# Indirect transfers of a routed mixture-of-experts kernel sent back to back: no spacing, no tile gates, three gather buffers, a last unit combined block by block

## What is computed

```python
x = x + 0.5 * ffn(layernorm(x))      # mixture of experts
x = x + attention(layernorm(x))      # RWKV mixing: projections, a scan over the 512 positions, a projection
x = x + 0.5 * ffn(layernorm(x))      # the same experts again
# ffn: softmax(x @ gate_w), the best 2 of 8 experts per token, their weights normalised, then for expert i
h = silu(x @ w1[i]) * (x @ w3[i])    # 128 -> 512
out += (h @ w2[i]) * weight_i        # 512 -> 128
```

## Time and profile before

| | us |
|---|---|
| median of three runs | 676.24 |
| lowest, highest | 674.56, 677.45 |
| the profiled execution | 672.78 |
| its span in the trace | 671.0 |
| PE busy / DVE busy / ACT busy / POOL busy | 528.1 / 412.7 / 319.7 / 297.2 |
| POOL idle before scatters, until an `h` gate opened (26 times) | 136.4 |
| POOL idle before gathers, until an `h` gate opened (21 times) | 27.4 |
| PE idle until an `h` was made (13 times) | 26.0 |
| DVE idle before combines, until a gather landed (14 times) | 63.3 |

### The profile page before, as it was taken

One profiled execution on the slowest core, in us unless ns is written; L12 is line 12 of the kernel. 1 busy time (PEld: TensorE's weight loads), 2 busy tenths in 40 slices (PEclk: granted clock), 3 DMA queues, 4 the chain that ended last, 5 costly groups with the idle time before them and its releaser, 6 DMA issues. The chain is left out here.

```text
span 671.0 us, 18790 instructions
## 1 busy us (share of the span) xinstructions
PE 528.1 (79%) x5866; PEld 482.5 (72%) x5866; DVE 412.7 (62%) x1218; ACT 319.7 (48%) x703; POOL 297.2 (44%) x499
## 2 busy tenths in 40 slices
PE   2136899993899889898999859989789999989500
PEld 1125799893788878677888749878789899879500
DVE  4845975221678789588897848859786443333311
ACT  5433754441484566654656615854645344334100
POOL 1270356666540550565405655046005555525543
PEclk9999999998799999998999959999799999999955
DMA  8943234442221221222211133111112324322311
GB/s 287 325 143 99 84 112 147 136 134 67 76 77 41 64 72 49 73 64 63 78 49 45 53 99 83 44 60 49 57 34 77 100 81 127 85 64 72 86 52 43
DMA packets 89016, 59.57 MB, mean 89 GB/s; under 512 B 10208, under 2 KB 82656, under 8 KB 88928
## 3 DMA queue, kind: packets, MB, share of 16 engines
q1 hardware_dynamic: 55248, 29.97, 15.3%
q0 software_dynamic: 8192, 16.79, 8.9%
q10 hardware_dynamic: 25488, 11.61, 5.9%
HBM read 28.65 MB, written 29.69 MB: 87 GB/s over the span
## 5 line engine op out<-in xcount | busy, mean ns | idle before, releaser
L694 POOL DMA_INDIRECT rows_in<-parts,slot x128 | 132.5, 1035 | 232.9 <-DVE h L1084 136.4
L1084 DVE TENSOR_TENSOR h<-sil,pb 128x512 f32<-128x512 f32 x177 | 120.9, 686 | 145.8 <-PE pb L1201 59.3
L1215 PE MATMUL py<-ffn_w,h 128*128 x1416 | 199.0, 284 | 13.6 <-ACT yrow L753 12.4
L1215 PEld LDWEIGHTS py<-ffn_w,h 128*128 128x128 f32 x1416 | 175.3, 195 | 20.0 <-issue 13.9
L1201 PE MATMUL pa<-rT,ffn_w 128*128 128x128 f16 (+1 forms) x1752 | 152.7, 234 | 36.8 <-DVE h L1084 26.0
L708 POOL DMA_INDIRECT yg<-rows_out,slot x128 | 123.8, 968 | 130.3 <-issue 53.6
L1201 PEld LDWEIGHTS pa<-rT,ffn_w 128*128 x1752 | 124.9, 100 | 52.6 <-issue 41.1
L1201 PE MATMUL pb<-rT,ffn_w 128*128 128x128 f16 (+1 forms) x1752 | 157.1, 233 | 0.1
L1201 PEld LDWEIGHTS pb<-rT,ffn_w 128*128 x1752 | 124.4, 99 | 7.6 <-issue 0.3
L768 ACT ACTIVATE sil<-pa 128x512 f32<-128x512 f32 x177 | 105.4, 595 | 42.6 <-PE pa L1201 32.8
L748 ACT ACTIVATE rT<-pT 128x512 f16<-128x512 f16 (+1 forms) x112 | 56.8, 508 | 92.5 <-PE pT L1188 81.2
(11 more groups left out here) (155 smaller groups left out, 442.0 us busy)
## 6 DMA issues: line engine op xcount, KB each, us to landing
rows_out<-yrow ACTq DMA_DIRECT2D x177, 64.0 KB
rin<-rows_in SPq DMA_DIRECT2D x65, 128.0 KB
rows_in<-zrow SPq DMA_DIRECT2D x34, 128.0 KB
shared<-in_w SPq DMA_DIRECT2D x16, 256.0 KB, 7.0
rin<-rows_in SPq DMA_DIRECT2D x47, 64.0 KB
rows_in<-zrow SPq DMA_DIRECT2D x2, 1472.0 KB, 12.2
xres<-in_x SPq DMA_DIRECT2D x4, 512.0 KB, 5.7
ffn_w<-in_w SPq DMA_DIRECT2D x8, 256.0 KB
```

Source lines behind the costliest of these rows:

```text
L694: pool.indirect_dma_start(rows_in[g][:], bass.IndirectOffsetOnAxis(ap=slot[:, c, at:at + 1], axis=0), parts[:, at, :], None).then_inc(s_sc ...
L1084: dve.tensor_tensor(h[:, t % RING, :], sil[:, t % 2, :], pb[t % 2][:], ALU.mult).then_inc(s_h, 1)
L1215: mm = pe.matmul(py[:], h[:, step % RING, at:at + T], w, start=(c == 0), stop=(c == FC - 1))
```

## The change

- `pace` is gone, and so are the gates: POOL sends the transfers in the order of `TRANSFERS`, as fast as it can. A transfer still waits for what it reads (slots, data, zero fill, stored results).
- `yg` has three buffers (`GSLOTS`), given out in the order of the gathers. The n-th unit waits for the combine of the (n-3)-th.
- The unit that comes last (D) is combined block by block: two gathers of a block land on a semaphore of their own, DVE adds them with two instructions, SP writes the 64 KB of this block.
- The costs of the planner are altered and the plan is built anew. Of 449 entries 134 keep their tile, most of the rest move by one tile, the furthest by four. The order of units in the gathers stays.

```diff
-UP, TURN, DOWN, COPY_T, COPY_Y, SILU, H = 0.67, 0.055, 0.92, 0.3, 0.28, 0.6, 0.69
-HOP, LAND, SEND, LOAD = 0.1, 4.0, 1.1, 3.0
-SLIP = {"dve": 6.0, "act": 3.1, "pe": 2.0}
-SPACE = 1.6
+UP, UP_ALONE, TURN, DOWN, COPY_T, COPY_Y, SILU, H = 0.66, 0.73, 0.055, 0.9, 0.3, 0.28, 0.6, 0.69
+HOP, LAND, SEND, LOAD = 0.1, 4.5, 1.1, 3.0
+SLIP = {"dve": 6.5, "act": 3.1, "pe": 1.4}
+SPACE = 1.55
...
-        yg = sb("yg", [P, UG, TOPK, JU, D])
+        yg = sb("yg", [P, GSLOTS, TOPK, JU, D])
...
+                    if (run, b) == GATHERS[-1]:
+                        for j in range(JU):
+                            sp.wait_ge(s_lastc, j + 1)
+                            sp.dma_start(ov[:, js, :][:, j, :], xres[:, js, :][:, j, :]).then_inc(s_out, 16)
+                        return
...
-                if (j, c) == (0, 0):
-                    before = [p[1:] for p in PLAN if p[1] == "gather" and p[3] == b]
-                    at_b = before.index(("gather", run, b))
-                    if at_b:
-                        pool.wait_ge(s_comb, count(("combine",), ("combine", before[at_b - 1][1], b)))
+                n = GATHERS.index((run, b))
+                if (j, c) == (0, 0) and n >= GSLOTS:
+                    pool.wait_ge(s_comb, count(("combine",), ("combine", *GATHERS[n - GSLOTS])))
...
-            for sent, (gate, name, *one) in enumerate(TRANSFERS):
-                wait(pool, s_h, gate)
-                wait(pool, s_pace, sent)
+            for _, name, *one in TRANSFERS:
                 if name == "scatter":
                     scatter(*one)
                 else:
                     gather(*one)
-                pool.memset(pace[:], 0).then_inc(s_pace, 1)
...
+            def combine_last(run, b):
+
+                u, js = units(run, b)
+                slot_ = (len(GATHERS) - 1) % GSLOTS
+                for j in range(JU):
+                    xj = xres[:, js, :][:, j, :]
+                    dve.wait_ge(s_last[j], 16 * TOPK)
+                    for c in range(TOPK):
+                        ins = dve.scalar_tensor_tensor(xj, yg[:, slot_, c, j, :],
+                                                       wts[:, c, u * JU + j:u * JU + j + 1], xj, ALU.mult, ALU.add)
+                        if c == 0:
+                            link(ins)
+                    ins.then_inc(s_lastc, 1)
```

More of the change, by code:

```diff
@@ L77 @@
 YSLOTS = 10
+GSLOTS = 3
 RING = 6
@@ L187, in tile @@
         q, half, _ = TILE_OF[t]
-        up1 = max(self.free["pe"], self.rT[q] + HOP, self.h.get(t - 2, 0.0) + HOP) + UP
+        up = UP if paired(t) else UP_ALONE
+        up1 = max(self.free["pe"], self.rT[q] + HOP, self.h.get(t - 2, 0.0) + HOP) + up
         if t > SKEW:
@@ L311, in ask, with in_use @@
         waiting.append([due, at, name, run, [(b, j, c) for b in units for j in range(JU) for c in range(TOPK)]])
+    def in_use(run, unit):
+        order = [p[2:] for p in plan if p[1] == "gather"]
+        n = order.index((run, unit))
+        return n >= GSLOTS and "combine" not in gathered[order[n - GSLOTS]].ends
     def send(tile, until):
         while True:
-            now = [w for w in waiting if w[1] <= until and not (w[2] == "gather" and any(
-                c.next() == "combine" for c in chains if c.unit == w[4][0][0] and gathered.get((c.run, c.unit)) is c
-                and c.run < w[3]))]
+            now = [w for w in waiting if w[1] <= until and not (w[2] == "gather" and in_use(w[3], w[4][0][0]))]
             at = max([free["pool"]] + [min((w[1] for w in now), default=until)])
@@ L385, in count @@
     return order.index(upto) + 1
+GATHERS = [p[2:] for p in PLAN if p[1] == "gather"]
 def run_of(t):
@@ L445, in macaron_kernel @@
         zrow = sb("zrow", [P, 2 * D], F16)
-        pace = sb("pace", [P, PACE], U8)
         e_desc = sb("e_desc", [P, JG, E])
@@ L558, in macaron_kernel @@
         s_yst = [sem(f"y_stored{i}") for i in range(YSLOTS)]
-        s_gat = [sem(f"gathered{b}") for b in range(UG)]
+        s_gat = [sem(f"gathered{i}") for i in range(GSLOTS)]
+        s_last = [sem(f"last_gathered{j}") for j in range(JU)]
+        s_lastc = sem("last_combined")
         s_comb = sem("combined")
@@ L665, in _ @@
             last_steps(step)
-            sp.wait_ge(s_out, 16 * B)
+            sp.wait_ge(s_out, 16 * (B - 1 + JU))
         @block.gpsimd
@@ L702, in gather @@
                         pool.wait_ge(s_yst[k], 16 * len(range(k, PEND[run], YSLOTS)))
[L703 to L707 removed]
+                n = GATHERS.index((run, b))
+                if (j, c) == (0, 0) and n >= GSLOTS:
+                    pool.wait_ge(s_comb, count(("combine",), ("combine", *GATHERS[n - GSLOTS])))
                 pool.indirect_dma_start(
[L709 to L710 removed]
+                    yg[:, n % GSLOTS, c, j, :], None, rows_out[SET[run]][0:PASS_STEPS[PASS[run]] * T, :],
+                    bass.IndirectOffsetOnAxis(ap=slot[:, c, at:at + 1], axis=0)).then_inc(
+                        s_last[j] if n + 1 == len(GATHERS) else s_gat[n % GSLOTS], 16)
             def every(run, units):
@@ L1088, in combine @@
                 u, js = units(run, b)
-                runs = [p[2] for p in PLAN if p[1] == "gather" and p[3] == b]
-                dve.wait_ge(s_gat[b], 16 * TOPK * JU * (runs.index(run) + 1))
+                n = GATHERS.index((run, b))
+                dve.wait_ge(s_gat[n % GSLOTS], 16 * TOPK * JU * (n // GSLOTS + 1))
                 for c in range(TOPK):
@@ L1106, in step @@
                 if name == "combine":
-                    combine(run, b)
+                    (combine_last if (run, b) == GATHERS[-1] else combine)(run, b)
                 if name in ("stats", "mstats"):
```

8 lines of the change are left out of this document (3 added, 5 removed).

## The result

| | us |
|---|---|
| before, median of four runs | 676.85 (674.56 to 677.63) |
| after, median of four runs | 868.48 (867.05 to 869.97) |
| ratio | 1.284, 95% interval 1.280 to 1.288 |
| the profiled execution of after, its span | 867.47, 865.7 |

What follows compares the result with a forecast made beforehand. The prediction took POOL's gathers to bound the end and PE's idle time the part before. Gains of 17.2 + 0.8 + 17 + 11.3 + 7.3 + 0 = 53.6 gave 619.2 for a profiled-like execution, 623 as median; range 609 to 643.

Steps and rivals of the forecast that it cites:

- Step 6: All POOL transfers sent at once, in bursts beside loads and stores: cost taken as 0, bounds 0 and +6 us.
- slower: Rival: bursts of transfers slow the loads and stores of the tiles, about 689 us; chance 0.03.
- Step 1: The tail: D's gathers wait only for tile 176's store, 17.2 us less; last block's combine and write, 0.8 less.
- The 0.8 for the last block: Behind the last gather: fewer DVE instructions and a smaller last write gain 0.8 us, bounds 0 and 2.2.
- Step 2: The stall after tile 34, where DVE and PE wait for run 0's gathers: 17 us saved, bounds 13 and 18.
- Step 3: Run 5: PE's wait for the first load, slow register load and low clock behind them; 11.3 us saved, bounds 4 and 14.
- The 4.5 for the register load: Run 5: the 7.2 us register load, beside seven loads landing at once, was to lose 4.5 us of excess.
- Steps 2 to 4 together: Stall after tile 34 (17), run 5 (11.3) and DVE's smaller waits for gathers (7.3): 35.6 us saved.
- Step 5: The new plan moves work by a tile or so: taken as 0, bounds -4 (gain) and +8 us.
- new stalls of PE with a fall of the clock: Sign that the forecast is wrong: such stalls standing between 175 and 475 us.
- Its sign for step 1: In the tail: D's gathers start 1.25 us apart, with 10 to 12 us between last store and last gather.
- its being locked out: Rival: POOL can't write descriptors where DVE is busy, 2.2 us per transfer, only the tail gained, 655 us; chance 0.05.

Runs made afterwards that it cites:

- e3: After, with a small memset behind each transfer that waits only for the memset before the last one (1.29 us between transfers); 876.77 us.
- e8: After, with a memset of 600 bytes behind each transfer, its wait long fulfilled (1.73 us between transfers); 642.26 us, ratio 0.953.
- e5: After, with the small memset, the wait for it and a second, long fulfilled wait before each transfer, no gates (1.87 us apart); 663.96 us, ratio 0.985.
- e17: After, with a 700-byte memset behind each transfer (1.81 us), none between the last ten, which wait for the last tile's h; 649.66 us, ratio 0.964.
- e16: After, with a 490-byte memset behind each transfer (1.64 us), none between the last ten, which wait for the last tile's h; 630.60 us, ratio 0.935.
- e14: After, with each of the 128 gathers replaced by a plain transfer of the same size from POOL, scatters still indirect; 615.54 us, executed once.
- e7: After, with the memset, the wait for it and the new plan's gates put back, so POOL's rules are those of before; 674.02 us, ratio 1.0024.
- e19: After, with the gathers replaced by plain transfers, scatters still indirect, run beside unchanged after on a chip that starves; 735.63 us.
- e9: After, with a memset of 380 bytes behind each transfer, its wait long fulfilled (1.55 us between transfers); 708.70 us.
- e10: After, with four transfers 1.25 us apart, then two long memsets, 1.72 us between transfers in the mean; 715.58 us.
- e13: After, with each scatter writing only the first 64 of its 128 rows, transfers back to back (1.20 us apart for scatters); 876.39 us.

## Why the prediction was wrong

**Step 6 failed.** It took 0 for sending at once, with bounds 0 and +6, because "nothing speaks for a loss". On the chips that starve it costs over 200 us: 868.48 against 642.26 for 1.73 us between transfers, and on one and the same chip 876.77 (e3) against 642.26 (e8). The step looked only at the transfers' bytes (the DMA share of 0.26). These are indeed no problem: in after the share in a burst is 0.20. What it should have asked is whether any row of before shows transfers 1.25 us apart beside a working PE. None does for long: in the burst of the earlier trace rows PE has nothing to do, and in the only other one, the scatters of run 0, it has almost nothing. The most work beside transfers so close is this, and it isn't slowed:

```profile
42.38 1.85 PE L1274 MATMUL bkB<-gate_w,xnT 128*128 128x8 f32 x8 [0.78 <-ACT xnT L805]
42.44 0.96 POOL L694 DMA_INDIRECT rows_in<-parts,slot  x1 [0.30 <-issue]
```

It lies at the third and fourth transfer of a row of eight, and in after PE falls off from the third to the fifth on (in the burst from 112.6 on it starts 12, 12, 18 and then 3 matmuls behind the first four transfers). So before could not show the loss, and the upper bound of +6 came from no row. The rival "slower" had the right trigger (bursts) but the wrong victim, and a chance of 0.03.

A page's rule, which the prediction did not use, points the same wrong way. The Trainium skill ("SBUF — State Buffer", section "SBUF: two separate sides") says that PE never waits on anyone for its side of SBUF and that transfers can't slow compute. PE slowed here all the same, so it was by another path than those ports, or the sentence is too wide.

The kernels in which PE is not starved tell how the other steps did.

**Step 1, right, 1.3 us too much.** 17.2 + 0.8 were forecast to be gained from the last store to the end. Before it took 671.0 - 631.96 = 39.0; after, by these rows, 865.7 - 843.39 = 22.3, so 16.7 less:

```profile
843.39 0.33 ACTq L768 DMA_DIRECT2D rows_out<-yrow  x1
846.51 0.95 POOL L719 DMA_INDIRECT yg<-rows_out,slot  x1 [33.50 <-issue]
...
855.26 0.95 POOL L719 DMA_INDIRECT yg<-rows_out,slot  x1 [0.30 <-issue]
...
857.85 0.74 DVE L1118 SCALAR_TENSOR_TENSOR xres<-yg,wts,xres 128x128 f32<-128x128 f32 x2 [1.68 <-DMA yg<-rows_out,slot]
```

Eight gathers take 8.75 as said; POOL starts 3.1 behind the store, not 2.6. The 0.8 for the last block is 0: from the last gather to the end it is 10.4 us in both kernels, what DVE saves is given back behind the last write.

**Step 2, right in its mechanism.** The wait after tile 34 follows POOL's pace: 15.0 us in e5 (1.87), 8.4 in e17 (1.81), 5.9 in e8 (1.73), 1.85 in e16 (1.64), none in e14. The row of e8:

```profile
159.72 2.31 DVE L1107 SCALAR_TENSOR_TENSOR xres<-yg,wts,xres 128x128 f32<-128x128 f32 x8 [5.94 <-DMA yg<-rows_out,slot]
```

In after this wait is gone too, but the burst of 24 that removes it costs a stall of 23.28 us at tile 29.

**Step 3, one term wrong.** PE's wait for the first load of run 5 (4.08 before) is gone in after, e8 and e16. The 4.5 for the register load was an error: I put the 7.2 us down to seven loads landing beside it. It is 7.1 in every kernel, on R with nothing starved as well, and where one load is issued beside it instead of seven (duration ns min/median/max of after, then of e14):

```profile
L1246 PEldq TENSOR_LOAD <-eid x9: 1042/1314/7147, 53.6 to 769.6; - x9
```

```profile
L1245 PEldq TENSOR_LOAD <-eid x9: 1045/1307/7125, 53.0 to 552.4; - x9
```

It belongs to the run with thirty registers.

**Steps 2 to 4 together, right in size.** They were to give 35.6 before the last store, 31.1 without the wrong 4.5. e14, with nothing starved, issues its last store 34.8 us sooner than before (597.21), though its gathers are quicker than those of after. e16, with 1.64 instead of 1.25 us, issues its last store at 601.75 instead of 631.96, 30.2 sooner:

```profile
601.75 0.33 ACTq L776 DMA_DIRECT2D rows_out<-yrow  x1
```

**Step 5, a loss of 5 inside its bounds.** With POOL as in before (e7), the new plan issues the last store at 636.99, 5.0 later, and DVE waits 16.1 after tile 34 instead of 13.1:

```profile
636.99 0.33 ACTq L773 DMA_DIRECT2D rows_out<-yrow  x1
```

The tail gives 4.2 of them back (34.8 us from the last store to the end instead of 39.0).

**The section "What would show it"** named the sign that came true: new stalls of PE with a fall of the clock between 175 and 475. Its sign for step 1 came true as well (11.9 us from the last store to the last gather in after). POOL's instructions did not grow (253.1 us for 267), so its being locked out is no part of this.

## What to carry to other kernels

A pause that seems to have no reader may protect an engine that shares no semaphore with it: before taking a spacing out, look whether the trace has one stretch where the unspaced form runs beside the engine that bounds the kernel, and if not, leave the cost unbounded above. In this kernel GpSimd's indirect transfers are best kept some 1.75 us apart (start to start) while TensorE works, evenly and not in groups, and may go back to back once it has ended. Measure such a change on more than one chip, and read the spacing from the timeline after each edit: one more wait instruction was 0.47 us here.

## What the runs showed of the hardware

- Indirect transfers of GpSimd 1.25 us apart bring TensorE down from some 10 matmuls a us to 1 or fewer, from the third to fifth transfer on and until 1 to 5 us after the last. In the longest hole one instruction comes each 0.7 or 1.4 us. The stalls are there whether the transfers gather or scatter, carry 128 rows or 64, and whether TensorE's addresses are fixed or not. TensorE's code arrives in time.
- Plain transfers of the same engine, 0.53 us apart with a DMA share of 0.61, do nothing of the kind (e19, on a chip that starves). The Trainium skill ("DMA: Bandwidth & Descriptors", section "SWDGE vs HWDGE vs iDMA") says that both kinds are put together by GpSimd's cores and go through descriptor rings in SBUF. The page of e19 agrees as far as it goes: with plain gathers this queue has the same 8192 packets and 16.79 MB as in after. So the number of packets and bytes in this queue is not the cause. It is something that goes with the indirect form; what the two forms write into the rings no run here shows.

```profile
q0 software_dynamic: 8192, 16.79, 7.5%
```

- The edge, between 1.55 and 1.73 us, lies where a transfer's first packet starts (in the packets of before, after, e8 and e9: 1.53 us after POOL's instruction at the earliest, 1.65 to 1.67 in the median). So it may be the overlap of two transfers in the making. That fits e10 and e13, but no run shows it, and e16 (1.64) was on the chip that doesn't starve.
- The starving differs between chips or loadings of a kernel (735.6 and 615.5 for one and the same kernel), while the kernel before is alike on all. Which of the two it is stays open, as does the path on which TensorE is held up.
